# Keys and values of the strided attention made within the warping stage, and the order of ScalarE's fills behind the warping norm

## The reference, cut to what matters

```python
x = x + _L1_ffn_ref(_layernorm(x, axis=-1), ...)                      # fourth block
x = x + _L2_xattn_ref(ctx_1024, _layernorm(x, axis=-1))               # fifth: warping
x = x + _L2_ffn_ref(_layernorm(x, axis=-1), ...)                      # sixth
x = x + _L3_xattn_ref(_layernorm(x, axis=-1), ctx_1024, ctx_1024, mask_BxS2_bf0, ...)   # seventh

# fifth, for each batch: small is the context (512 rows), large is the normed x (256 rows)
D = _pairwise_euclidean(small, large)      # sqrt(max(aa + bb - 2ab, 0))
R = _dtw_cost(D)                           # r = d + min(up, left, diagonal), row by row
i_idx, j_idx, valid = _backtrack(R, T_small, T_large)
expanded = zeros.at[j_idx].add(small[i_idx] * valid)

# seventh: head width 8, 16 heads
k = (key @ Wk + bk)        # key and value are the context: they don't depend on x
v = (value @ Wv + bv)
scores = einsum(q, k) * SCALE
scores = where((s_idx - h_idx) % 4 != 0, -inf, scores)
scores = where(key_padding_mask, -inf, scores)
context = einsum(softmax(scores), v)
return context @ Wo + bo
```

## Time and profile before

| | |
|---|---|
| median of 3 runs | 1169.76 us (1166.8 to 1170.95) |
| profiled execution | 1171.81 us |
| its span, first to last instruction | 1170.0 us |
| PE busy | 920.3 us, 79% |
| DVE busy | 690.2 us, 59% |
| ACT busy | 472.7 us, 40% |
| POOL busy | 5.9 us, 1% |
| mean granted TensorE clock | 0.831 of 2.4 GHz |

### The profile page before, as it was taken

How to read it: one execution, slowest core, us unless ns; L and a number is a source line. 1 busy time by engine, 2 the same in 40 slices (tenths; PEclk the granted TensorE clock), 3 DMA queues, 4 the chain that set the end, 5 groups by cost and what they waited for, 6 DMA issues and landing times. The chain is left out here.

```text
span 1170.0 us, 16897 instructions
## 1 busy us (share of the span) xinstructions
PE 920.3 (79%) x5993; PEld 566.7 (48%) x5996; DVE 690.2 (59%) x2640; ACT 472.7 (40%) x1110; POOL 5.9 (1%) x25
## 2 busy tenths in 40 slices
PE   5999998499999999996888863557011697899798
PEld 3666665356566656654445533223000532466437
DVE  3656555556656566565455518999999445445232
ACT  3655554555555555553124434112122153223340
POOL 0000000000000000000000000000000100000000
PEclk8999999689999999997578956788555779678578
DMA  8610000000000000000000000000000000000000
GB/s 247 124 45 2 1 1 1 0 1 1 1 1 1 1 1 1 1 1 1 1 1 2 1 1 2 1 1 0 1 1 1 1 1 0 1 1 1 1 0 18
DMA packets 25460, 13.65 MB, mean 12 GB/s; under 512 B 12954, under 2 KB 23714, under 8 KB 25379
## 3 DMA queue, kind: packets, MB, share of 16 engines
q1 hardware_dynamic: 25378, 12.59, 4.3%
HBM read 12.06 MB, written 0.52 MB: 11 GB/s over the span
## 5 line engine op out<-in xcount | busy, mean ns | idle before, releaser
L437 ACT ACTIVATE wide_probs<-PS,wide_nmax 128x512 f32<-128x512 f32 (+2 forms) x256 | 140.4, 556 | 48.8 <-DVE wide_nmax L362 48.8
L362 DVE TENSOR_REDUCE wide_nmax<-PS 128x2 f32<-128x1024 f32 (+2 forms) x128 | 113.7, 889 | 35.9 <-PE PS L307 26.0
L307 PE MATMUL PS<-wide_kT,wide_qT 64*128 64x512 f32 (+2 forms) x512 | 112.8, 519 | 1.9 <-ACT wide_kT L431 1.9
L320 PE MATMUL PS<-constants,wide_probs 128*128 128x128 f32 x704 | 102.1, 279 | 0.0
L285 PE MATMUL PS<-wide_pT,wide_v 128*64 128x256 f32 (+1 forms) x768 | 90.2, 370 | 0.2 <-DVE wide_v L357 0.2
L320 PEld LDWEIGHTS PS<-constants,wide_probs 128*128 128x128 f32 x704 | 78.7, 142 | 18.8 <-ACT wide_probs L437 11.7
L443 ACT COPY wide_pT<-PS 128x512 f32<-128x512 f32 (+2 forms) x128 | 57.8, 451 | 45.4 <-PE PS L320 45.4
L368 DVE COPY wide_pT<-PS 128x512 f32<-128x512 f32 (+2 forms) x128 | 66.2, 517 | 2.6
L1496 PE MATMUL PS<-w_up_or_diagonal,constants 128*128 128x512 f32 (+2 forms) x44 | 28.9, 746 | 47.4 <-DVE w_up_or_diagonal L1635 47.4
L285 PEld LDWEIGHTS PS<-wide_pT,wide_v 128*64 128x64 f32 x768 | 49.6, 136 | 29.4 <-issue 10.4
L866 DVE TENSOR_REDUCE l1f_nmax<-PS 128x4 f32<-128x1024 f32 x32 | 39.2, 1226 | 41.5 <-PE PS L1188 41.4
(11 more groups left out here) (417 smaller groups left out, 1766.8 us busy)
## 6 DMA issues: line engine op xcount, KB each, us to landing
ctx_by_lane<-ctx_dram SPq DMA_DIRECT2D x4, 256.0 KB, 7.1
top_w<-L_ffn_W_dram SPq DMA_DIRECT2D x2, 512.0 KB
constants<-constants_dram SPq DMA_DIRECT2D x1, 679.0 KB, 5.8
x<-x_dram SPq DMA_DIRECT2D x1, 512.0 KB, 4.7
l0x_wq<-L_xattn_Wq_dram SPq DMA_DIRECT2D x1, 512.0 KB, 8.5
l0x_wk<-L_xattn_Wk_dram SPq DMA_DIRECT2D x1, 512.0 KB, 5.2
l0x_wv<-L_xattn_Wv_dram SPq DMA_DIRECT2D x1, 512.0 KB, 7.2
l0x_bv<-L_xattn_bv_dram SPq DMA_DIRECT2D x1, 512.0 KB, 5.3
```

The source lines that it names most:

```text
L307: mm = pe.matmul(PS[:, self.S[qt][h], 0:self.keys(qt)], w.qT[rows, n % 2, qt * P:qt * P + P], w.kT[rows, n % 2, 0:self.keys(qt)], start=Tr ...
L320: mm = pe.transpose(PS[:, self.T[h], kt * P:kt * P + P], w.probs[:, qt, h, kt * P:kt * P + P], ident)
L362: v.tensor_reduce(w.nmax[:, (2 * n + qt) % 4, :], PS[:, self.S[qt][0]:self.S[qt][1] + 1, 0:self.keys(qt)], AX.X, ALU.max, negate=True).the ...
L437: act.activation(w.probs[:, qt, h, 0:self.keys(qt)], PS[:, self.S[qt][h], 0:self.keys(qt)], ACT.Exp, bias=w.nmax[:, (2 * n + qt) % 4, h:h ...
```

## The change: what it does, and the diff

Keys and values of the seventh stage are made in the warping stage. After the last key of the way back is written (`keyed`), TensorE runs `tensor_early`: for every batch two key products with their mask rows and a value product of four small parts, through PSUM banks 0 to 3 in turn, and at the end the bias of the values times the output weights, added to the output bias. ScalarE takes each in `scalar_early`, between `scalar_keys` and `scalar_cells`. The value bias is no longer added to the values but to x by way of that product. The padding that GpSimd did is done by ScalarE in `scalar_pad`, between `scalar_distances` and `scalar_keys`, and `vector_padding` moves into `vector_distances`, ahead of the shuffle of the context. The values are projected with the unpadded weights, and their zeros and ones are written once. `tensor_first`, the four other key projections and the four value projections of the seventh stage go, with `take_k` and `take_v` there. The buffers for keys, values and padded weights of `l3x` are now placed below those of the warping stage. The value bias is loaded as a column.

In the warping stage ScalarE does only the turned context between the root and the copy of `yT`; zeros and identities come after the squares, zeros first. TensorE waits for the turned context only from the fifth product group on.

```diff
@@ NarrowAttention
-            return (use("m", 1, b) + use("ot", 1, b - 1) + use("q", 0, b + 2) + use("k", 0, b + 3) + use("at", 0, b - 1) + use("m", 0, b + 1)
-                    + use("ot", 0, b) + use("out", 0, b - 1) + use("v", 0, b + 1) + use("k", 1, b + 3))
+            return (use("m", 1, b) + use("ot", 1, b - 1) + use("q", 0, b + 2) + use("at", 0, b - 1) + use("m", 0, b + 1)
+                    + use("ot", 0, b) + use("out", 0, b - 1))
...
+    def scalar_pad(self, act):
+
+        zero = self.k.cst[:, C_ZERO:C_ZERO + 1]
+        act.wait_ge(self.loaded, self.n_loads)
+        for w in (self.wq, self.wk):
+            act.copy(w[:, :], zero.to_broadcast((P, 2 * P))).then_inc(self.zeroed, 1)
+        for rows in (self.nmax[:, :, :, :, :].rearrange("p q t g e -> p (q t g e)"), self.v[:, :, :].rearrange("p b c -> p (b c)")):
+            act.copy(rows, zero.to_broadcast((P, rows.shape[1]))).then_inc(self.rows_set, 1)
+        act.wait_ge(self.zeroed, 4)
+        for i, w in ((0, self.wq), (1, self.wk)):
+            act.copy(w[:, :].rearrange("p (j e) -> p j e", e=32)[:, :, 0:2 * D8],
+                     self.w_in[:, i, :].rearrange("p (j e) -> p j e", e=2 * D8)).then_inc(self.padded, 1)
+        act.wait_ge(self.rows_set, 2)
+        ones = self.v[:, :, D8::32]
+        act.activation(ones, zero.unsqueeze(1).to_broadcast((P, B, ones.shape[2])), ACT.Copy, bias=1.0).then_inc(self.rows_set, 1)
+        act.copy(self.bv_wide[:, :], self.bv_col[:, 0:1].to_broadcast((P, P))).then_inc(self.rows_set, 1)
+
+    def tensor_early(self, pe):
+
+        PS, k = self.k.PS, self.k
+        pe.wait_ge(self.padded, 2)
+        pe.wait_ge(self.rows_set, 4)
+        pe.wait_ge(self.cls_sb, 3)
+        for n, (kind, i, b) in enumerate(self.early):
+            if n >= 4:
+                pe.wait_ge(*self.taken(self.early[n - 4]))
+            bank = PS[:, n % 4, :]
+            if kind == "k":
+                self.key_product(pe, bank, i, b)
+                self.key_rows(pe, bank, b).then_inc(self.k_ps, 1)
+            else:
+                for j in range(4):
+                    mm = pe.matmul(bank[:, 32 * j:32 * j + 32].rearrange("p (q e) -> p q e", q=4), k.ctxT[:, b, j::4],
+                                   self.w_in[:, 2, :].rearrange("p (q j e) -> p j q e", q=4, j=4)[:, j, :, :], start=True, stop=True)
+                mm.then_inc(self.v_ps, 1)
+        pe.matmul(PS[:, 6, 0:P], self.bv_wide[:, :], self.wo[:, :], start=True, stop=False)
+        pe.matmul(PS[:, 6, 0:P], k.ident, self.bo[:, :], start=False, stop=True).then_inc(self.bo_ps, 1)
+
+    def scalar_early(self, act):
+
+        for n, (kind, i, b) in enumerate(self.early):
+            bank = self.k.PS[:, n % 4, :]
+            if kind == "k":
+                act.wait_ge(self.k_ps, self.nk * b + i + 1)
+                act.activation(self.kp[:, b, i, :], bank, ACT.Identity, bias=self.bkp[:, i:i + 1]).then_inc(self.k_sb, 1)
+            else:
+                act.wait_ge(self.v_ps, b + 1)
+                act.copy(self.v[:, b, :].rearrange("p (k e) -> p k e", e=32)[:, :, 0:D8],
+                         bank[:, 0:P].rearrange("p (k e) -> p k e", e=D8)).then_inc(self.v_sb, 1)
+        act.wait_ge(self.bo_ps, 1)
+        act.copy(self.bo[:, :], self.k.PS[:, 6, 0:P]).then_inc(self.bo_sb, 1)
...
@@ vector_first
-        v.wait_ge(self.loaded, self.n_loads)
+        v.wait_ge(self.bo_sb, 1)
...
@@ tensor, period b
                 if b + 2 < B:
                     self.q(pe, b + 2)
-                if b + 3 < B:
-                    self.project_keys(pe, 0, b + 3)
                 scores(2, b)
...
                 if behind:
                     output(b - 1)
-                if ahead:
-                    values(b + 1)
-                if b + 3 < B:
-                    self.project_keys(pe, 1, b + 3)
...
@@ Warping
+    def scalar_turn(self, act):
+
+        act.copy(self.ctxTr[:, :, :].rearrange("p b s -> p (b s)"), self.k.ctxT[:, :, :].rearrange("p b s -> p (b s)")[:, ::-1]).then_inc(self.turned_round, 1)
...
@@ tensor_distances
-                pe.wait_ge(self.filled, 4)
+                pe.wait_ge(self.ones_set, 1)
...
             if h >= 4:
                 pe.wait_ge(self.d2_done, h - 3)
+                pe.wait_ge(self.turned_round, 1)
...
@@ scalar_distances
         act.activation(self.sq[:, :], self.k.yT[:, :], ACT.Square).then_inc(self.sq_done, 1)
-        act.wait_ge(self.filled, 4)
+        self.scalar_fill(act)
+        act.wait_ge(self.filled, 2)
...
@@ gpsimd
-            l3x.pool_pad(pool)
-            l3x.pool_rows(pool)
...
@@ tensor
             l2x.tensor_keys(pe)
+            pe.wait_ge(l2x.keyed, len(l2x.KEY_CUTS) - 1)
+            l3x.tensor_early(pe)
             l2x.tensor_cells(pe)
...
-            l3x.tensor_first(pe)
             ln.tensor_transpose(pe, 7, 6)
...
@@ scalar
-            l2x.scalar_fill(act)
+            l2x.scalar_turn(act)
             ln.scalar_yT(act, 4)
             l2x.scalar_distances(act)
+            l3x.scalar_pad(act)
             l2x.scalar_keys(act)
+            l3x.scalar_early(act)
             l2x.scalar_cells(act)
...
-            l3x.scalar_first(act)
             ln.scalar_yT(act, 6)
...
@@ vector
-            l2x.vector_distances(v)
+            l2x.vector_distances(v, l3x.vector_padding)
...
-            l3x.vector_padding(v)
             l2f.vector(v)
```

102 lines of the change are left out of this document (31 added, 71 removed).

## The result

The changed kernel takes 1150.24 us (median of 4 runs, 1148.2 to 1157.05) against 1168.28 for the kernel before (4 runs): a ratio of 0.9854, 95% interval 0.9807 to 0.9901. On a second chip it was 1148.91 (6 runs) against 1170.61 (11 runs), ratio 0.9803 (0.9766 to 0.9840). The ratios leave out runs over 1.5% above the fastest of their kernel: of this one a run of 1598.08 us at a clock of 0.739 on the second chip, and three of the six runs of the first experiment. The forecast was 1152.1, in a range of 1143 to 1162.

What follows compares the result with a forecast made beforehand. TensorE's products between units were taken to bound the seventh stage's loop, VectorE's two chains the warping stage. 4.24 + 13.75 + 1.3 - 1.7 = 17.6 us gave 1154.2 profiled, 1152.1 as median; range 1143 to 1162.

Steps and rivals of the forecast that it cites:

- The head of the seventh stage: Start of the seventh stage: without four key products queries start 5.19 us earlier but run colder; gain 4.24 us.
- Period -1: Seventh stage's loop: unit 2 follows the queries (1.64 us), unit 0 of the next period follows VectorE's maximum (2.19 us).
- Period 0: Seventh stage's loop: unit 2 and the next period start right behind VectorE's maximum, gaining 1.57 and 3.13 us.
- Periods 1 and 2: Seventh stage's loop: only value products go; the next periods start 2.61 us (maximum) and 2.86 us (exponential) earlier.
- The head of the warping stage: Start of the warping stage: yT and column sums come earlier, partly offset by mask row and small additions; gain 1.3 us.
- Work counted as nothing: Early block (26 us if uncovered), ScalarE's padding (5.6 us), GpSimd's fills, loop copies and column load: no cost or gain.
- The clock: Seventh stage's loop: 5 us more at half clock than the mix gives, charged at 1.7 us lost.
- the mix: Seventh stage's loop: share of half clock as before, 58 of 97 us, so 50 of 83 us after the change.
- Colder loop: Seventh stage's loop: stays mostly at half clock without dense products, 8 to 13 us lost, 1158 to 1163; chance 0.21.
- Warmer loop: Seventh stage's loop: nearly all at full clock like the fourth stage, 10 to 17 us more gain, 1135 to 1143; chance 0.11.
- Hidden anyway: Loop's freed gaps fill with another wait, only the two heads gain 5.5 us, 1164 to 1165; chance 0.03.
- Slower chains: Warping stage's 316 slots slow from moved buffers or busy neighbours; 70 ns a slot gives 1174; chance 0.03.

Runs made afterwards that it cites:

- the first experiment: Kernel before with only ScalarE's order at the warping stage's start changed (norm copies and squares first, fill next): 1168.1 us against 1168.0, six runs.
- the kernel with the head alone: Kernel before with only the keys of batches 0 and 1 made in the warping stage, their padding moved too: 1162.69 us, ratio 0.9956.
- the filled loop: Changed kernel with TensorE's key and value products put back in the seventh stage's loop, results taken by nobody: 1154.75 us, ratio 0.9895.
- the head filled: Changed kernel with four key products ahead of the turning of y at the seventh stage's head, results taken by nobody: 1156.61 us, ratio 0.9904.
- the delay: Changed kernel with two VectorE additions (1.2 and 0.6 us) at the very end of the warping stage, results taken by nobody: 1154.56 us, ratio 0.9877.

## Why the prediction was right, point by point

**The head of the seventh stage** (4.24): 4.27, with queries of 2.07 us at half clock as assumed, and 4.27 again in the kernel with the head alone.

**Period -1** (1.64 + 2.19): 3.96 against before and 4.10 against the filled loop. Unit 2 starts behind the queries and unit 0 behind the maximum, as written.

**Period 0** (1.57 + 3.13 = 4.70): 3.76. Two things in this step were off. Unit 2 doesn't start right behind the maximum: the query products begin at the same time and, at half clock, end 0.84 us after it (1028.37 - 1027.53). In the kernel before the same products were mostly at full clock and ended at 1034.55, just ahead of the maximum's 1034.63:

```profile
1033.29 1.26 PE L1088 MATMUL PS<-yT,l3x_wq 128*128 128x256 f32 x4
```

The forecast left them out of this step, so the 0.84 is a cost of where the half clock stood. And a handoff at the start of a period takes 0.15 to 0.25 us; the 0.05 put in is that of the units within a period. 4.70 - 0.84 - 0.25 is 3.6.

**Periods 1 and 2** (2.61 + 2.86): -0.86 and 2.72 as they stand. They aren't at like clocks: period 1 went from 1.00 to 0.71. The same loop with the head filled ran it in 16.00 us at 0.84, against 17.55 at 0.71. That is 5.1 and 10.2 us at half, so 0.30 us for each. At full clock period 1 would be 17.55 - 3.1 = 14.5, a gain of 2.2. Period 2 has 6.7 us at half instead of 8.6, which gives 0.6 of its 2.72 to the clock. By this estimate the two are worth 4.3 instead of 5.47.

**The head of the warping stage** (1.3): 1.75 in the stage, and 1.95 for the order of fills alone, so the mask row on VectorE costs 0.2. The column sums came at 6.39 us, 6.65 was forecast, since the small instructions ahead of the shuffle overlap.

**Work counted as nothing.** The early block took 23.1 us where 26 were put, and ended at 842.7 where 845 was. ScalarE's padding cut its wait from 18.95 to 14.96 us, so 4.0 where 5.6 was put. The cells were caught up by 854.6 where 860 was put. Made twice the block is still free, and made three times it costs 17.5. The copies in the loop count as nothing, as forecast. The fills that GpSimd no longer makes reached 0.8 us into the writing of y in the sixth stage, and that went from 2.16 us to 2.14: no gain to speak of. The Trainium skill, in SBUF — State Buffer, section on who interferes with whom, has VectorE and GpSimd lock a shared pair of ports only for some forms of VectorE's instructions, a tensor_scalar in a two-port mode among them. The prediction took it without that condition, and whether the writing of y meets it no view here shows.

**The clock** (-1.7) is the term that was wrong, in size and sign, without moving the total much. The loop's mean of 0.71 is inside the 0.55 to 0.85 that the forecast allowed. But the half clock fell otherwise than the mix assumed. The tail, which has no product less, took 6.90 us less at 0.95 instead of 0.57. With period 1's loss of 3.1 and period 2's gain of 0.6 the clock brought 4.4 us in the seventh stage. In the sixth stage it took 2.41 back, and the eighth, untouched and at 0.81 instead of 0.79, was 1.75 shorter. The forecast looked at the loop alone, at one mean clock, and so had the tail wrong and missed the other two stages.

**The sum.** Terms without the clock: 4.27 + 3.96 + 3.76 + 2.2 + 2.15 = 16.3 in the seventh stage where 18.0 were forecast. The clock adds 4.4, and the stage gains 20.75. With 1.75 from warping, -2.41, 1.75 and -0.14 that is the 21.7 of the two profiles. The medians say 18.0 on one chip and 21.7 on the other, for 17.6 forecast.

So the mechanism held, and the closeness of the total is in part luck. The parts without the clock brought 18.1 us (16.3 and 1.75) where 19.3 were forecast, and the clock some 3.7 where -1.7 was; the 0.84 of period 0 is still among the first. How little the clock's part belongs to the change shows in the seventh stage of kernels in which TensorE does the same there: 89.4 us with the early block three times, 91.8 in the changed kernel, 99.3 with the delay. The forecast gave no reason for the 91.8 of both profiles of the changed kernel, and no run shows what sets it.

**The rivals.** *Colder loop*: did not occur, 0.71 after 0.70 with TensorE's busy share down from 92% to 89%. The Trainium skill, in TensorE: Matmul & The Clock Gate, section on the HAM clock gate, has activity release the clock. The trace only half agrees: the filled loop was indeed warmer (1.00 and 0.90 in periods 1 and 2), but TensorE also stood at 0.50 for 10.3 us in which it was busy throughout. *Warmer loop*: not as a whole, though its tail was. *Hidden anyway*: out, by the filled loop. *Slower chains*: out, the scans of both chains take 284 to 289 ns, with one block, two and three.

## What to carry to other kernels

Work that doesn't depend on the running data is best moved beside a long dependent chain on another engine, and the room there can be worked out from when its last product is needed: here between 50 and 77 us, by estimate 60. When a product between two units goes, look at what stood just ahead of it: its end, at the clock of that place, is the next bound, and the handoff behind it was 0.05 to 0.25 us here. Judge an edit of a few us by the stages that it touches, against the same stage of several kernels, before believing its total.

## What was not expected of the hardware

- A stage of 1023 identical products took 158.2 us or 164.4 at granted clocks of 0.77 and 0.73, in kernels that don't differ there. A tail of some 109 products took 16.4 or 23.3 (0.95, 0.57), and both lengths came in kernels with the same work in the whole stage.
- The granted clock was at its lower level while TensorE was busy without a gap, for 6.8, 10.3 and 13.6 us in the sixth stage.
- Dense dummy products ahead of a stage brought its head to full clock (queries 1.13 us instead of 2.07), and the half clock then stood in the tail of the stage, 60 us later: 1 us gained and 6.6 lost.
- A us at half clock costs between nothing (period 0 took 16.66 us at 0.59 and 16.65 at 0.50) and 0.38 us (the tail, 6.9 us for 18.4). It depends on whether TensorE is what the period waits for.
